# Experts of a decoder layer: result transposed, down weights in two parts, summed in PSUM, gates multiplied into silu's output

## The chip, the cores and the metric

One core of one Trainium2 chip runs the whole kernel. The metric is device time in microseconds (us). Five engines work beside each other and meet at semaphores: PE (TensorE, matmuls; PEld is its weight load), DVE (VectorE), ACT (ScalarE), POOL (GpSimd) and SP (SyncE, which here only issues DMAs). Each engine takes its instructions strictly in the order in which they were written.

## The reference, cut to what matters

One decoder layer for 8 batches of 256 tokens with 128 features: self attention, cross attention to 512 context tokens, then a mixture of experts, each followed by a residual and a layer norm. Only the experts change:

```
probs = softmax(xf @ w_router); top_vals, top_idx = top_k(probs, 2)
gates = top_vals / sum(top_vals);  cw = scatter(gates over 8 experts)
h1 = xf @ w1[e]; h3 = xf @ w3[e]                  # 128 -> 256, 8 experts
y  = (silu(h1) * h3) @ w2[e]                      # 256 -> 128
out = sum_e cw[:, e] * y[e] + (silu(xf @ sw1) * (xf @ sw3)) @ sw2
x = layernorm(x + out)
```

The kernel computes all experts for all tokens and weights them with gates, of which all but two are zero. The shared expert (sw1, sw3, sw2) is number 0, the routed ones are 1 to 8, so there are NE = 9 per batch and 72 in all.

## The kernel before, in words

The self attention of all batches comes first, then the cross attention, then the experts, batch by batch. What an engine does is recorded by `emit(kind, b, par, i)`, and an `Order` sets the sequence: every kind has a due time within a batch, counted in experts, and an engine's instructions are sorted by it. The experts' stage has its Orders in `experts` (from L1206) and is started from the engines' blocks in `decoder_layer`.

An expert step before is this. PE does kind H: twelve matmuls (L1463 to L1465) of 128x256 in fp32r, which give h1 and h3 transposed (hidden on the partitions, 256 tokens on the free axis). Every product is made of three, since the up weights and the tokens are each held as a rounded part and a rest ("hi" and "lo", fp32r). ACT takes silu of h1 (L1333), DVE multiplies by h3 (L1411) into `hidden`. PE does kind Y, two experts later (LAG = 2): four matmuls (L1472) of 128x128 in fp32, two tiles of 128 tokens times two halves of the hidden axis (eight records in the trace, since each runs in two passes), with `hidden` as the stationary operand and `w_down` as the moving one, so that y has tokens on the partitions. DVE then adds y to `state`: the shared expert by L1423, each routed one by L1425, which multiplies by the token's gate (a scalar per partition). PSUM has three slots of two banks, and H and Y take them by turns.

After the ninth expert of a batch DVE takes statistics (L1431), POOL computes mean and root in a chain of twelve small instructions (L1287 to L1305, kind TAIL, in an Order of its own), DVE normalizes (L1403, kind NORM), and SP stores. POOL has nothing else to do in the stage but for its beginning: there it makes the rests of the up weights of experts 3 to 8 (L1276, kind UP) and the chain of the cross attention's last layer norm (L819 to L841, kind N3). The top-2 choice (kind ROUTE, 18 DVE instructions with one ACT exp in between, L1327) is made once for batches 0 to 6 during the last cross attention and once for batch 7 in the experts' first two batches.

Of the kernel before, what the change touches and what calls it, by code (L numbers as in the profile page):

```python
# [123 lines left out]
def decoder_layer(nc, x, ctx, mask, wq, wk, wv, wo, g1, b1, g2, b2, xwq, xwkv, xwout,  # L124
# [28 lines left out]
    with top:  # L153
# [45 lines left out]
        m.room, m.powers = early.vals, early.powers  # L199
# [15 lines left out]
        with nc.Block() as block:  # L215
# [8 lines left out]
            @block.gpsimd  # L224
            def _(pool):
                emit, more = c.gpsimd(pool), e.gpsimd(pool)
                a.gpsimd(pool, {last: steps(emit, "N1", 5, 0, 1) + steps(emit, "N2", 5, 9, 1),
                                B: steps(emit, "Y", 1, 9, 1)})
                c.pool_order.run(emit, {1: steps(more, "UP", r.FIRST, 3, 2)}, done=("N1", "N2", "Y"),
                                 left=[("N3", last), ("XLO", last)])  # L230
                for at in range(r.FIRST, r.FIRST + 2):
                    more("UP", 0, 0, at)
                for at in range(5):
                    emit("N3", last, last % 2, at)
                for at in range(r.FIRST + 2, NE):
                    more("UP", 0, 0, at)
                more("XLO", last, last % 2, 0)
                e.tail_order.run(more)

            @block.scalar  # L240
            def _(act):
                emit, more = c.scalar(act), e.scalar(act)
                a.scalar(act, {B: steps(emit, "TX", 1, 5, 1) + steps(emit, "TC", 1, 5, 1)})
                c.act_order.run(emit, {1: steps(more, "UP", r.FIRST, 2, 2), last: steps(more, "EXP", 1, 27, 1), B: steps(more, "H", r.AHEAD, 5, 1)},
                                done=("TX", "TC"))
                for at in range(r.FIRST, NE):
                    more("UP", 0, 0, at)
                e.order.run(more, left=ahead, between={0: [(6.75, lambda: more("XT", last, last % 2, 0))], 1: [(0.5, lambda: more("EXP", 1, 0, 0))]})

            @block.vector  # L250
            def _(dve):
# [16 lines left out]
            @block.tensor
            def _(pe):
# [3 lines left out]
                e.order.run(more, left=ahead, between={0: [(6.5, lambda: more("XT", last, last % 2, 0)), (8, lambda: more("LOGITS", last, last % 2, 0))]})  # L273
# [3 lines left out]
def between_stages(nc, sem, sb, mem, m):  # L277
# [21 lines left out]
    r.gates = sb(mem, "gates", [P, tiles, E])  # L299
# [394 lines left out]
def cross_early(mem, sb, m):  # L694
# [5 lines left out]
    e.ctx_in = sb(mem, "ctx_in", [P, 2, CT, D])  # L700
# [5 lines left out]
    e.normed = sb(mem, "normed", [P, KT, D])  # L706
    e.y = sb(mem, "y", [P, KEYS])
# [9 lines left out]
def cross_attention(nc, sem, sb, ps, slot, m, r, mem, early, last_use):  # L717
# [173 lines left out]
    def scalar(act):  # L891
        def emit(kind, b, par, i):
            if kind in ("TC", "TX") and b < B:
# [5 lines left out]
                                     scale=gb[:, g:g + 1], bias=gb[:, g + 1:g + 2]).then_inc(ready, 1)  # L899
            if kind == "TX" and b >= 2:  # L900
# [289 lines left out]
    c.heads_ready = heads_ready, B * PAIRS  # L1190

# [10 lines left out]
def experts(nc, sem, sb, ps, slot, m, r, c, mem):  # L1202
# [41 lines left out]
    slots = Turns(order, full, SLOTS, c.free)  # L1244
# [263 lines left out]
```

## Time and profile before

| | us |
|---|---|
| median of 3 runs | 1153.52 (1153.27 to 1154.64) |
| the profiled execution | 1154.32 |
| its span in the trace | 1152.5 |
| PE busy in the span | 1104.0 (96%) |
| DVE, ACT, POOL busy | 879.1, 735.5, 539.6 |
| granted TensorE clock, mean | 0.996 of full speed |

Times of rows count from the span's start. A matmul's duration in the trace holds its way through the array, and matmuls overlap: what one costs is the distance from its start to the next start. A group's row gives the mean duration of one. An instruction's duration on DVE or POOL also holds the time in which it has been started and cannot go on.

### The profile page before, as it was taken

The page shows a single profiled execution, that of the slowest core. Times are in us where ns is not written, and L with a number is a line of the kernel's source. Part 1 is how long each engine was busy: PE and PEld are TensorE (multiplying, and loading weights), DVE is VectorE, ACT ScalarE, POOL GpSimd, SP SyncE. Part 2 cuts the span into 40 slices and gives each one's busy share as a digit, 9 for nine tenths or more (in the row PEclk, how much of TensorE's full clock was granted, in tenths as well). Part 3 has the DMA queues.
Part 4 walks back from the last instruction along what each step waited for, and adds up shares of the span by engine and source line. Part 5 has one row for each costly group of instructions (what it writes and reads, how often), then busy time and mean ns, then how long its engine had stood idle before and what let it go on. Part 6 is the DMA issues. An engine that isn't in the chain of part 4 may idle for free. (4 is left out here: it accounts for less than half of the span.)

```text
span 1152.5 us, 27526 instructions
## 1 busy us (share of the span) xinstructions
PE 1104.0 (96%) x8781; PEld 946.9 (82%) x8781; DVE 879.1 (76%) x2786; ACT 735.5 (64%) x1754; POOL 539.6 (47%) x892
## 2 busy tenths in 40 slices
PE   6999997999999999999999999999999998999997
PEld 5888875778888887887888888888788887999997
DVE  7999996888878788778787878877878685655554
ACT  6999996667757666666765766666667565322221
POOL 4666665554574355446456445544644432400101
PEclk9999999999999999999999999999999999999999
DMA  2000011000000000000000000000000003000000
GB/s 92 7 7 11 7 44 38 1 11 1 2 1 11 2 1 11 1 1 11 2 1 1 11 2 1 2 1 2 1 2 1 2 1 96 3 10 6 11 6 11
DMA packets 14685, 12.39 MB, mean 11 GB/s; under 512 B 1361, under 2 KB 13649, under 8 KB 14417
## 3 DMA queue, kind: packets, MB, share of 16 engines
q1 hardware_dynamic: 14128, 10.43, 3.0%
q8 instruction: 75, 1.23, 0.4%
q14 instruction: 66, 0.53, 0.2%
q10 hardware_dynamic: 416, 0.20, 0.1%
HBM read 9.57 MB, written 1.05 MB: 9 GB/s over the span
## 5 line engine op out<-in xcount | busy, mean ns | idle before, releaser
L874 POOL TENSOR_TENSOR xk_parts<-k_raw,xk_parts 64x768 fp32r<-64x768 f32 x128 | 236.1, 1845 | 312.7 <-DVE xk_parts L992 310.0
L1016 DVE CUSTOM_DVE_ANT_0 xmasked<-ps,bar 128x768 f32<-128x768 f32 x256 | 244.3, 954 | 4.2 <-issue 0.6
L1128 PE MATMUL ps<-xk_parts,xq_parts 128*128 128x512 f32 (+1 forms) x1024 | 233.2, 350 | 6.9 <-DVE xq_parts L997 3.4
L929 ACT ACTIVATE xprobs<-xmasked,xlow 128x768 f32<-128x768 f32 x256 | 238.0, 930 | 1.4 <-DVE xlow L1016 1.4
L1134 PE MATMUL ps<-ident,xprobs 128*128 128x128 f32 x1536 | 215.0, 276 | 7.1 <-DVE xlow L1016 6.0
L1128 PEld LDWEIGHTS ps<-xk_parts,xq_parts 128*128 128x128 f32 x1024 | 174.4, 189 | 33.3 <-DVE xq_parts L997 3.8
L1134 PEld LDWEIGHTS ps<-ident,xprobs 128*128 128x128 f32 x1536 | 168.9, 140 | 16.7 <-DVE xlow L1016 10.8
L1145 PE MATMUL ps<-xprobs_t,xvals 128*64 128x256 f32 x1536 | 179.9, 383 | 1.1 <-ACT xprobs_t L935 1.1
L1145 PEld LDWEIGHTS ps<-xprobs_t,xvals 128*64 128x64 f32 x1536 | 104.8, 137 | 57.9 <-issue 10.6
L1021 DVE COPY xprobs_t<-ps 128x768 f32<-128x768 f32 x128 | 121.6, 950 | 3.5 <-PE ps L1134 3.5
L909 ACT ACTIVATE k_raw<-ps 128x768 f32<-128x768 f32 x64 | 52.0, 812 | 105.1 <-PE ps L1102 94.3
L1333 ACT ACTIVATE xvals<-ps 128x512 f32<-128x512 f32 x72 | 42.9, 597 | 115.4 <-PE ps L1465 114.2
L115 DVE MEMSET xspare<- 128x1 f32 x256 | 15.1, 59 | 132.8 <-issue 111.4
L497 ACT ACTIVATE probs<-masked,low 128x128 f32<-128x128 f32 (+1 forms) x256 | 114.6, 458 | 0.0
L935 ACT ACTIVATE xprobs_t<-ps 128x768 f32<-128x768 f32 x128 | 103.0, 805 | 4.1 <-PE ps L1134 2.6
L1411 DVE TENSOR_TENSOR xvals<-ps,xvals 128x512 f32<-128x512 f32 x72 | 49.7, 691 | 69.0 <-ACT xvals L1333 69.0
L941 ACT ACTIVATE xrsum_t<-ps 128x256 f32<-128x256 f32 x64 | 24.6, 385 | 112.1 <-PE ps L1153 112.1
L451 POOL TENSOR_TENSOR q_head<-q_parts,head_of 128x256 fp32r<-128x256 f32 x128 | 76.2, 613 | 31.5 <-DVE q_parts L560 31.5
L570 DVE CUSTOM_DVE_ANT_0 masked<-ps,causal 128x128 f32<-128x128 f32 (+1 forms) x256 | 79.5, 353 | 0.0
L921 ACT ACTIVATE xvals<-ps 128x768 f32<-128x768 f32 x64 | 52.0, 812 | 41.0 <-PE ps L1120 41.0
L1472 PE MATMUL ps<-w_down,xvals 128*128 128x128 f32 x576 | 75.9, 275 | 1.1 <-DVE xvals L1411 1.1
L1472 PEld LDWEIGHTS ps<-w_down,xvals 128*128 128x128 f32 x576 | 70.2, 191 | 1.5 <-DVE xvals L1411 1.5
(220 smaller groups left out, 2524.8 us busy)
## 6 DMA issues: line engine op xcount, KB each, us to landing
ctx_in<-in_ctx SPq DMA_DIRECT2D x8, 256.0 KB, 3.3
w_rest<-in_L_ffn_w SPq DMA_DIRECT2D x2, 768.0 KB, 6.4
raw_kv<-in_L_xattn_Wkv SPq DMA_DIRECT2D x1, 1024.0 KB, 5.3
out<-state SPq DMA_DIRECT2D x8, 128.0 KB, 2.0
x_in<-in_x SPq DMA_DIRECT2D x7, 128.0 KB, 2.2
raw_q<-in_L_xattn_Wq SPq DMA_DIRECT2D x1, 512.0 KB, 6.1
wout<-in_L_xattn_Wout SPq DMA_DIRECT2D x1, 512.0 KB, 3.9
keep_all<-in_mask_BxS_bk SPq DMA_DIRECT2D x1, 512.0 KB, 4.7
```

Of the source, the lines that this page charges most:

```text
L451: pool.tensor_tensor(q_head[:, i % 4, :], q_parts[:, g % 2, :].bitcast(F32), head_of[:, i % HG:i % HG + 1].broadcast_to([P, S]), ALU.mult) ...
L497: nc.scalar.activation(probs[:, i % 4, lo:hi], masked[:, r, lo:hi], ACT.Exp, scale=-1.0, bias=low[:, r, j:j + 1], accum_out=sums[:, g % 2, ...
L570: dve.tensor_tensor_reduce(masked[:, r, lo:hi], bank(s, hi - lo, j * S), causal[:, S - (hi - lo):S], 1.0, 3e38, ALU.add, ALU.min, low[:, r ...
L874: pool.tensor_tensor(k_parts[dst, i // 2 % 2, h, :], k_raw[src, :], k_parts[src, i // 2 % 2, h, :].bitcast(F32), ALU.subtract).then_inc(k_ ...
L929: nc.scalar.activation(probs[:, i % 4, :], masked[:, i % 4, :], ACT.Exp, scale=-1.0, bias=low[:, i % 4:i % 4 + 1], accum_out=sums[:, pair ...
L935: nc.scalar.activation(probs_t[:, i % 4, :, 0, :], slot(slots.place("PT", 2 * i), KEYS).rearrange("p (k t) -> p k t", k=KT), ACT.Copy).the ...
L1016: dve.tensor_tensor_reduce(masked[:, i % 4, :], slot(slots.place("S", i), KEYS), bar[:, par, :], 1.0, 3e38, ALU.add, ALU.min, low[:, i % 4 ...
L1021: dve.tensor_copy(probs_t[:, i % 4, :, 1, :], slot(slots.place("PT", 2 * i + 1), KEYS).rearrange("p (k t) -> p k t", k=KT)).then_inc(pt_dv ...
L1128: last = nc.tensor.matmul(slot(s, hi - lo, lo), q_parts[:, pair % 2, h, part, t * P:(t + 1) * P], k_parts[:, pair % 2, h, lo:hi], start=pa ...
L1134: last = nc.tensor.transpose(slot(s, P, j * P), probs[:, i % 4, j * P:(j + 1) * P], ident[:, :])
L1145: last = nc.tensor.matmul(ps[h * XD:(h + 1) * XD, O_BANK + i % 2, 0:S], vals[:, i // 2 % 2, j, c:c + XD], probs_t[:, (2 * i + h) % 4, j, : ...
L1472: last = nc.tensor.matmul(slot(s, D, j * D), hidden[:, i % 3, k * S + j * P:k * S + (j + 1) * P], w_down[:, i, k, :], start=(k == 0), stop ...
```

## The change

The result of an expert is now transposed: `w_down` is the stationary operand, `hidden` the moving one, in fp32r in three products as H has them, so Y is six matmuls of 128x256. For that `w_down` and `hidden` are each split in a rounded part and a rest: the weights once (kind DOWN, ACT L1408 and DVE L1508), hidden for every expert (kind HI on ACT, L1433, and kind LO on DVE, L1522). All nine experts of a batch add up in one PSUM bank; then ACT copies the sum out (SUM, L1437), PE transposes it back (BACK, L1606), and DVE adds it to `state` (ADD, L1529), once per batch.

A gate per token can no longer be a scalar per partition. So the gates are transposed by PE, written to DRAM, and read back broadcast to all partitions (`load_wide`, 1 MB per batch, into the rooms of the attention's `k_parts` and `q_parts`), and POOL multiplies them into silu's output before DVE's H multiplies by h3 (kind GATE, L1361). The shared expert has no GATE. In batch 7 the shared expert comes last.

The choice is now made for batches 0 to 5 and for 6 and 7. Y's lag is three experts. TAIL is cut in five pieces that stand among the GATEs. The rests of the up weights of experts 3, 5, 7 are made by DVE, those of 4, 6, 8 by POOL. `w_down` is loaded earlier, during the last cross attention, into the room of `ctx_in`, `normed` and `y`.

```diff
-    LAG = 2
-    order = Order(B, NE, {"H": (NE, 0), "Y": (NE, LAG)})
-    dve_order = Order(B, NE, {"H": (NE, 0), "Y": (NE, LAG), "NORM": (1, NE + LAG + 2.25)})
-    tail_order = Order(B, NE, {"TAIL": (1, NE + LAG + 2.5)})
+    LAG = 3
+    END = NE + LAG
+    order = Order(B, NE, {"H": (NE, 0), "Y": (NE, LAG), "BACK": (1, END + 1.5)})
+    dve_order = Order(B, NE, {"H": (NE, 0), "LO": (NE, 0.95), "ADD": (1, END + 1.9), "NORM": (1, END + 5.9)})
+    act_order = Order(B, NE, {"H": (NE, 0), "HI": (NE, 1.5), "SUM": (1, END + 0.6)})
+    pool_order = Order(B, NE, {"GATE": (NE, 0.75), "TAIL": (5, END + 2.8, 0.65)})
...
+    def load_wide(sp, b):
+        sp.wait_ge(rows_written, 16 if b < r.EARLY else 32)
+        if b < 2:
+            sp.wait_ge(*c.scored)
+        else:
+            sp.wait_ge(weighted, E * (b - 1))
+        wait(sp, loaded_wide, 16 * b)
+        n = E * T
+        sp.dma_start(wide[b % 2], r.gate_rows[b * n:(b + 1) * n, :].rearrange("(e t) p -> e (t p)", e=E).partition_broadcast(P)
+                     ).then_inc(loaded_wide, 16)
...
+            if kind == "GATE" and expert(b, i) > 0:
+                n, e = b * NE + i, expert(b, i)
+                pool.wait_ge(silu_done, n + 1)
+                pool.wait_ge(loaded_wide, 16 * (b + 1))
+                values = silu[:, i % RING, :].rearrange("p (k s) -> p k s", k=HB)
+                pool.tensor_tensor(values, values, wide[par][:, e - 1:e, :].broadcast_to([P, HB, S]), ALU.mult
+                                   ).then_inc(weighted, 1)
...
+            if kind == "HI":
+                act.wait_ge(hidden_ready, n + 1)
+                wait(act, y_full, n - RING + 1)
+                nc.scalar.activation(hidden_hi[:, i % RING, :], hidden[:, i % RING, :], ACT.Copy).then_inc(hi_done, 1)
+            if kind == "SUM":
+                act.wait_ge(y_full, (b + 1) * NE)
+                nc.scalar.activation(summed_t[:, par, :], ps[:, O_BANK + par, 0:S], ACT.Copy).then_inc(sum_out, 1)
...
             if kind == "H":
                 dve.wait_ge(silu_done, n + 1)
-                wait(dve, full["Y"], n - 2)
-                dve.tensor_tensor(hidden[:, i % 3, :], slot(s, HB * S, BANK),
-                                  silu[:, i % 3, :], ALU.mult).then_inc(hidden_ready, 1)
-            if kind == "Y":
-                for j in range(T):
-                    tokens, y = state[:, b * T + j, :], slot(s, D, j * D)
...
-                        dve.scalar_tensor_tensor(out=tokens, in0=y, scalar=gates[:, b * T + j, i - 1:i], in1=tokens,
-                                                 op0=ALU.mult, op1=ALU.add).then_inc(summed, 1)
+                if expert(b, i) > 0:
+                    dve.wait_ge(weighted, weights_before(b, i))
+                wait(dve, split, n - RING + 1)
+                dve.tensor_tensor(hidden[:, i % RING, :], slot(s, HB * S, BANK),
+                                  silu[:, i % RING, :], ALU.mult).then_inc(hidden_ready, 1)
+            if kind == "LO":
+                dve.wait_ge(hi_done, n + 1)
+                wait(dve, y_full, n - RING + 1)
+                dve.tensor_tensor(hidden_lo[:, i % RING, :], hidden[:, i % RING, :],
+                                  hidden_hi[:, i % RING, :].bitcast(F32), ALU.subtract).then_inc(split, 1)
+            if kind == "ADD":
+                dve.wait_ge(back_full, b + 1)
+                dve.tensor_tensor(tokens, ps[:, O_BANK + par, S:S + T * D].rearrange("p (t d) -> p t d", t=T), tokens,
+                                  ALU.add).then_inc(summed, 1)
...
             if kind == "Y":
-                for j in range(T):
-                    for k in range(HB):
-                        last = nc.tensor.matmul(slot(s, D, j * D),
-                                                hidden[:, i % 3, k * S + j * P:k * S + (j + 1) * P],
-                                                w_down[:, i, k, :], start=(k == 0), stop=(k == HB - 1))
+                pe.wait_ge(down_ready, i + 1 if b == 0 else NE)
+                pe.wait_ge(split, n + 1)
+                o = ps[:, O_BANK + par, 0:S]
+                for k in range(HB):
+                    nc.tensor.matmul(o, wh, xh, start=(i == 0 and k == 0), stop=False)
+                    nc.tensor.matmul(o, wh, xl, start=False, stop=False)
+                    last = nc.tensor.matmul(o, wl, xh, start=False, stop=(i == NE - 1 and k == HB - 1))
```

How the instructions stand on POOL in an ordinary batch of the experts' stage before; the names are the small statistics of the layer norm, and the next batch's chain follows at once:

```order
L1287 TENSOR_TENSOR n_gap<-n_stats 128x2
L1288 TENSOR_TENSOR n_var<-n_stats 128x2
L1289 TENSOR_TENSOR n_sum<-n_stats 128x2
L1291 TENSOR_TENSOR n_fix<-n_gap 128x2
L1292 TENSOR_SCALAR n_var<-n_var 128x2
L1293 TENSOR_SCALAR n_mean<-n_sum 128x2
L1295 TENSOR_TENSOR n_var<-n_var,n_fix 128x2
L1297 TENSOR_TENSOR n_root<-n_var,x_powers 128x2
```

POOL in an ordinary batch of the change (`xvals` is the room of silu's output, `xq_parts` and `xk_parts` the rooms of the broadcast gates; L1361 is GATE):

```order
L1361 TENSOR_TENSOR xvals<-xvals,xq_parts 128x512 x5
L1369 TENSOR_TENSOR n_gap<-n_stats 128x2
L1370 TENSOR_TENSOR n_var<-n_stats 128x2
L1371 TENSOR_TENSOR n_sum<-n_stats 128x2
L1374 TENSOR_TENSOR n_fix<-n_gap 128x2
L1375 TENSOR_SCALAR n_var<-n_var 128x2
L1376 TENSOR_SCALAR n_mean<-n_sum 128x2
L1378 TENSOR_TENSOR n_var<-n_var,n_fix 128x2
L1361 TENSOR_TENSOR xvals<-xvals,xq_parts 128x512
L1381 TENSOR_TENSOR n_root<-n_var,x_powers 128x2
L1361 TENSOR_TENSOR xvals<-xvals,xq_parts 128x512
L1384 TENSOR_TENSOR n_fix<-n_root 128x2
```

The chain of the batch before now stands between the GATEs of experts 5 to 8, and what is queued behind a GATE waits for it. DVE in the middle of a batch before, from one expert to the next, with the end of the batch before it (statistics, first expert's addition):

```order
L1411 TENSOR_TENSOR xvals<-ps,xvals 128x512
L1425 SCALAR_TENSOR_TENSOR state<-ps,gates,state 128x128 x2
L1429 MEMSET n_spare 128x1
L1431 BN_STATS n_stats<-state 128x6 x2
L1411 TENSOR_TENSOR xvals<-ps,xvals 128x512
L1423 TENSOR_TENSOR state<-ps,state 128x128 x2
```

DVE at the same place of the change (L1516 is H, L1522 LO with `y_hi` and `y_lo` as the rooms of hidden's two parts, L1529 ADD):

```order
L1516 TENSOR_TENSOR xvals<-ps,xvals 128x512
L1529 TENSOR_TENSOR state<-ps,state 128x256
L1532 MEMSET n_spare 128x1
L1534 BN_STATS n_stats<-state 128x6 x2
L1522 TENSOR_TENSOR y_lo<-xvals,y_hi 128x512
L1516 TENSOR_TENSOR xvals<-ps,xvals 128x512
L1522 TENSOR_TENSOR y_lo<-xvals,y_hi 128x512
```

The two gated additions of every expert are gone, and an expert's LO stands between its own H and the next one's, so DVE's next H cannot start before ACT's HI and the LO of the expert before are done. The beginning of the stage on DVE in the change (L1503 makes rests of up weights, L1508 those of down weights, L1061 adds the cross attention's result):

```order
L1516 TENSOR_TENSOR xvals<-ps,xvals 128x512
L1503 TENSOR_TENSOR rest_lo<-w_rest,rest_hi 128x2x256
L1522 TENSOR_TENSOR y_lo<-xvals,y_hi 128x512
L1061 TENSOR_TENSOR state<-ps,state 128x256
L1065 BN_STATS stats<-state 128x6 x2
L1508 TENSOR_TENSOR down_lo<-front,down_hi 128x256 x2
L1516 TENSOR_TENSOR xvals<-ps,xvals 128x512
L1503 TENSOR_TENSOR rest_lo<-w_rest,rest_hi 128x2x256
L1508 TENSOR_TENSOR down_lo<-front,down_hi 128x256
L1522 TENSOR_TENSOR y_lo<-xvals,y_hi 128x512
```

Twelve weight splits stand among DVE's work of the first batch, where there were none.

## Rows read from the trace of the kernel before

**Rows 1.** The page, part 1: busy us, share of span, instructions
```profile
PE 1104.0 (96%) x8781; PEld 946.9 (82%) x8781; DVE 879.1 (76%) x2786; ACT 735.5 (64%) x1754; POOL 539.6 (47%) x892
```

**Rows 2.** Windows of one batch: length, busy by engine, clock, DMA
```profile
1024.90:1045.45 20.55, 20.55 (x182) 20.55 (x182) 11.73 (x33) 5.37 (x9) 2.80 (x12) 1.00 0.03 8
...
1107.15:1127.72 20.57, 20.57 (x183) 20.57 (x182) 11.75 (x33) 5.37 (x9) 2.80 (x12) 1.00 0.03 8
```

**Rows 3.** Chain that ended last: start, us, what; Y's of three batches
```profile
982.27 0.90 PE ps L1472 x8
...
1024.89 0.90 PE ps L1472 x8
...
1045.45 0.90 PE ps L1472 x8
```

**Rows 4.** Timeline of PE, one H and its neighbours: start, us
```profile
987.67 0.28 PE L1464 MATMUL ps<-cxt_lo,rest_hi 128*128 128x256 f32 x1
...
988.92 1.05 PE L1472 MATMUL ps<-w_down,xvals 128*128 128x128 f32 x8
```

**Rows 5.** Groups, 960 to the end: count, busy us, mean ns, idle before
```profile
L1411 DVE TENSOR_TENSOR xvals<-ps,xvals 128x512 f32<-128x512 f32 x72 | 49.7, 691 | 69.0 <-ACT xvals L1333 69.0
L1333 ACT ACTIVATE xvals<-ps 128x512 f32<-128x512 f32 x72 | 42.9, 597 | 115.4 <-PE ps L1465 114.2 <-issue 1.2
L1276 POOL TENSOR_TENSOR rest_lo<-w_rest,rest_hi 128x512 fp32r<-128x512 f32 x6 | 7.5, 1276 | 9.7 <-ACT rest_hi L1318 9.7
L1318 ACT ACTIVATE rest_hi<-w_rest 128x512 fp32r<-128x512 f32 x6 | 3.2, 616 | 0.2 <-issue 0.2
```

**Rows 6.** Groups of POOL over the whole span, one input broadcast
```profile
L451 POOL TENSOR_TENSOR q_head<-q_parts,head_of 128x256 fp32r<-128x256 f32 x128 | 76.2, 613 | 31.5 <-DVE q_parts L560 31.5
```

**Rows 7.** Timeline of POOL and DVE, two pairs that overlap
```profile
988.61 1.27 POOL L1276 TENSOR_TENSOR rest_lo<-w_rest,rest_hi 128x512 fp32r<-128x512 f32 x1
988.66 1.30 DVE L1050 TENSOR_SCALAR state<-state,r_mean,r_root 128x128 f32<-128x128 f32 x1
...
950.04 1.84 POOL L874 TENSOR_TENSOR xk_parts<-k_raw,xk_parts 64x768 fp32r<-64x768 f32 x1 [3.56 <-DVE xk_parts L992]
951.58 0.44 DVE L1361 TENSOR_TENSOR scratch<-scratch,index 128x112 f32<-128x112 f32 x1
```

**Rows 8.** Timeline of DVE, a like instruction with POOL idle
```profile
954.26 0.27 DVE L1365 TENSOR_TENSOR chosen<-index,first 128x112 f32<-128x112 f32 x1
```

**Rows 9.** Timeline, a small POOL instruction behind a DVE cast
```profile
334.19 0.55 DVE L992 CAST xk_parts<-k_raw 64x768 fp32r<-64x768 f32 x1
...
334.23 0.56 POOL L828 TENSOR_TENSOR r_var<-r_var,r_fix 128x2 f32<-128x2 f32 x1
```

**Rows 10.** Chain that ended last, the last batch's end
```profile
1141.37 0.04 issue
1141.42 0.60 ACT xvals L1333
...
1142.79 2.07 PE ps L1472 x16
1144.94 0.61 DVE state L1425 x2
...
1146.15 0.20 POOL n_gap L1287
...
1149.66 0.35 DVE state L1403
```

**Rows 11.** Timeline of ACT around the second choice
```profile
999.60 1.28 ACT L1327 ACT_TABLE_LOAD   x1
...
1001.32 1.28 ACT L1333 ACT_TABLE_LOAD   x1
```

**Rows 12.** The page, part 6: DMA issues, KB each, us to landing
```profile
raw_kv<-in_L_xattn_Wkv SPq DMA_DIRECT2D x1, 1024.0 KB, 5.3
```

More of the change, by code:

```diff
@@ new lines, in _ @@
+                e.dve_order.run(more, left=ahead[:1] + [("LO", 0, 0)], between={
+                    0: [(0.5 + 0.5 * i, lambda i=i: more("DOWN", 0, 0, i)) for i in range(NE)]
+                    + [(at, lambda i=i: more("UP", 0, 0, i)) for i, at in ((5, 1.2), (7, 3.2))],
+                    1: [(7.5, lambda: emit("NORM2", last, last % 2, 0))],
+                    2: [(7.25, lambda: more("XHI", last, last % 2, 0)),
+                        (8.25, lambda: more("LOGITS", last, last % 2, 0))],
+                    3: [(0.5 + 0.3 * n, lambda n=n: more("ROUTE", 1, 0, n)) for n in range(r.STEPS)]})
@@ L272, in _ @@
                 c.pe_order.run(emit, {B: steps(more, "H", r.AHEAD, 2, 1)}, done=("TX", "TC"))
-                e.order.run(more, left=ahead, between={0: [(6.5, lambda: more("XT", last, last % 2, 0)), (8, lambda: more("LOGITS", last, last % 2, 0))]})
+                e.order.run(more, left=ahead, between={
+                    2: [(6.5, lambda: more("XT", last, last % 2, 0)), (8, lambda: more("LOGITS", last, last % 2, 0))],
+                    4: [(7, lambda: more("GATES", 0, 0, 0))]})
         e_mem.close()
@@ L298, in between_stages @@
     r.gate = sb(mem, "gate", [P, 2, tiles])
[L299 removed]
+    r.gates = sb(mem, "gates", [P, B, E, T])
+    r.gates_t = sb(mem, "gates_t", [P, 2, P])
+    r.gate_rows = nc.dram_tensor("gate_rows", [B * E * T, P], F32, kind="Internal").ap()
+    r.EARLY = 6
+    r.chain, r.gates_out = sem("r_chain"), sem("r_gates_out")
     r.moments = [sb(mem, "r_" + n, [P, T]) for n in ("gap", "total", "var", "fix", "mean", "root")]
@@ L899, in emit @@
                                      scale=gb[:, g:g + 1], bias=gb[:, g + 1:g + 2]).then_inc(ready, 1)
+            if kind == "TX" and b == B:
+                act.wait_ge(full["TX"], b + 1)
+                rows = r.EARLY * E * T
+                nc.scalar.activation(r.gates_t[0:rows, 0, :], slot(slots.place("TX", 0), P)[0:rows, :], ACT.Copy
+                                     ).then_inc(r.gates_out, 1)
             if kind == "TX" and b >= 2:
@@ L1080, in emit @@
                     last = nc.tensor.transpose(slot(s, P, n * P), normed[:, j, :], ident[:, :])
+            if kind == "TX" and b == B:
+                pe.wait_ge(r.chain, r.STEPS)
+                nc.tensor.transpose(slot(s, P)[0:r.EARLY * E * T, :],
+                                    r.gates[:, 0:r.EARLY, :, :].rearrange("p b e t -> p (b e t)"), ident[:, :])
             if kind == "TX" and b >= 2:
@@ L1380, in route @@
             if n == 17:
-                last = dve.tensor_tensor(gates[:, tiles, :], chosen[:, 0, tiles, :], chosen[:, 1, tiles, :], ALU.add)
-            last.then_inc(chain, 1)
+                first_b, end_b = (n // T for n in groups[g])
+                one, two = (chosen[:, k, tiles, :].rearrange("p (b t) e -> p b e t", t=T) for k in range(2))
+                last = dve.tensor_tensor(gates[:, first_b:end_b, :, :], one, two, ALU.add)
+            last.then_inc(r.chain, 1)
         def emit(kind, b, par, i):
```

290 lines of the change are left out of this document (179 added, 111 removed).

## The prediction

> **What bounds the kernel now.** I read the shares by engine first, then windows of single batches, then the chain that ended last, and then the groups of the experts' stage. PE is busy for 96% of the span [rows 1]. In the experts' stage it is all of the time: in two batches far apart PE is busy for 20.55 of 20.55 and 20.57 of 20.57 us at a granted clock of 1.00, while DVE has 11.7 us, ACT 5.4 and POOL 2.8 [rows 2]. The chain confirms it: the first batch's Y of expert 0 starts at 982.27, that of the third at 1024.89, the fourth's at 1045.45 [rows 3]. At 20.57 per batch the first pair would be 41.14 apart; it is 42.62, so 1.5 us of waits stand in the first two batches, and from there on a batch costs what PE works. So less work on PE is worth its full price, but only for as long as what feeds PE keeps up. Before, ACT and DVE stand between an H and its Y, and both are idle more than half of the time; the change puts POOL among them and gives DVE and ACT a second turn.
>
> **PE's work.** Eleven matmuls of an H take 988.92 − 987.67 = 1.25 us, 0.114 each, and a Y 0.90 [rows 3, 4]. After, Y is six matmuls of H's shape: 6 × 0.117 = 0.70 (0.114 is measured; the stationary operand of half of them differs, so I take up to 0.119). 72 × (0.90 − 0.70) = 14.4 us less. BACK adds two transposes per batch, at most H's price each: 16 × 0.11 = 1.8. Net −12.6 us, between −13.7 and −11.5 for a Y of 0.68 to 0.71. A batch would be 20.57 − 1.8 + 0.22 = 19.0 us, an expert 12 × 0.114 + 0.70 = 2.07.
>
> **What feeds PE.** Durations [rows 5]: silu 0.60; DVE's H 0.69; HI, an ACT copy of 128x512, 0.62 as the one of L1318; LO on DVE, of H's size, 0.69; GATE on POOL, as the subtraction of 128x512 at L1276, 1.28, or 1.24 back to back. GATE's second input is broadcast, and POOL's 128x256 with such an input takes 0.61 [rows 6], twice that 1.23; so 1.24, and 1.04 as a lower bound if the fixed part of it is 0.2. Per batch: POOL 8 × 1.24 + 3.5 of TAIL (1146.15 to 1149.66, [rows 10]) = 13.4; DVE 9 × 1.38 and the additions and norm, below 15; ACT 9 × 1.22 + a SUM of at most 0.60, 11.6. None of it is over 19.0. The sums do not bind; what can is the order.
>
> Two loops matter. First, PE's H of expert i+3 needs the PSUM slot of i, which DVE's H frees. From the end of H(i) to there PE has three Y and two H, 2.1 + 2.74 = 4.8 us; silu takes 0.64 of it, and 4.1 are left for GATE 1.24, DVE's H 0.69 and, with hops and a DVE that is just at the LO before, about 2.6 in all. The slack is 1.5 us. Y(i) has H(i+3) more, 1.37, for HI and LO, about 1.4: the same slack. Second, LO(i) stands on DVE ahead of H(i+1), and waits for ACT's HI(i): 0.69 + 0.62 + 0.69 and two hops are about 2.05 per expert. That is PE's own 2.07, so a lag that has once arisen is not worked off by DVE.
>
> **Whether DVE and POOL disturb each other.** GATE reads two operands from SBUF, and so does LO; DVE's H reads one from PSUM. The trace has such pairs. A DVE instruction on SBUF that started 0.05 after POOL's L1276 took 1.30 and ended 0.09 after it. A TENSOR_TENSOR of DVE with two SBUF inputs took 0.44 behind POOL's L874 and ended 0.13 after that [rows 7], where one of its kind took 0.27 with POOL idle [rows 8]. So DVE waits for POOL. The other way, a POOL instruction of 128x2 started at 334.23 beside a DVE cast and took 0.56, to 0.05 after the cast's end [rows 9], against 0.20 for such an instruction [rows 10]. That was a cast, not a two-input operation; no row has POOL starting under one of those. I take it that LO holds POOL as the cast did: for its elements, (0.69 − 0.27) / 400 = 1.05 ns each, 512 of them 0.54 us.
>
> The Trainium skill (SBUF — State Buffer, "Who interferes with whom") says that a DVE instruction with two SBUF inputs and a GpSimd instruction that reads SBUF share a port pair, which the first to start keeps until its end. The rows above agree where DVE comes second (1.30 and 0.44); for the case that POOL comes second behind a two-input DVE operation no row of this trace shows it, and by that page the sum is the one that follows, with the hold both ways.
>
> **An ordinary batch.** Between the end of GATE 5 and that of GATE 8 POOL has three GATEs and nearly all of TAIL, since its pieces stand among them: 3 × 1.24 + 3.5 = 7.2, and three LOs that hold it, 3 × 0.54 = 1.6, so 8.9 us. PE takes 6.2 for three experts. The 2.7 of excess less the slack of 1.5 leaves 1.2 us of idle PE per batch, which the DVE loop does not give back, over seven batches with a TAIL before them: +8.4. POOL itself does recover, in GATEs 1 to 4. Bounds: 0 if nothing is held, 1.9 per batch (+13) if hops cost more slack.
>
> **The first batches.** Twelve weight splits stand among DVE's work of batch 0: nine DOWN of 128x256 (elements 0.27, with the fixed part 0.42) and three UP of LO's size; POOL makes three UP, 3.7 us. What excludes each other in that batch is GATEs 9.9, POOL's UP 3.7, LOs 9 × 0.54 = 4.9, DOWN 9 × 0.27 = 2.4 and DVE's UP 1.6: 22.5 against 19.0, 3.5 too much; 1.5 more for the DVE loop, which has the splits in its way even with the port free: +5. Bounds: 1.5 with nothing held; 7 with whole durations held (0.69 and 0.42), which makes 25.7. In batch 1 POOL makes the layer norm of the cross attention's last batch, a chain like TAIL: +1. In batch 3 DVE makes the second choice, 18 small instructions, while ACT loads its table twice, 1.28 each [rows 11], and silu and HI are late by 2.6 at one blow, over a slack of 1.5: with DVE's 18 beside it +2.5 (bounds 1 and 4). Before, these cost 1.5 in batches 0 and 1, which goes.
>
> **The end.** Before, from the last H to the end of the sum it is 1141.37 to 1145.55, 4.2 us [rows 10]. After, batch 7 ends with the shared expert, without GATE, but expert 7's GATE comes about 1 late, then H, HI, LO of expert 7 (2.05), the same of expert 8 (2.05), Y 0.70, SUM 0.4, BACK 0.23, ADD 0.42 and hops 0.6: 7.5, so +3.3.
>
> **Costed at nothing.** The broadcasts are 1 MB per batch. A load of 1 MB landed in 5.3 us [rows 12], under 19 of a batch, with DMA at 3% [rows 2]; a batch's load starts when the GATEs two batches back are done. The load of w_down and the first gates' way through DRAM lie in the last cross attention, where DVE's and PE's work covers them. If the first broadcast were late, GATE(1) of batch 0 would stop everything once by what is missing.
>
> **Sum.** −12.6 + 8.4 + 5 + 1 + 2.5 + 3.3 − 1.5 = +6.1. The profiled execution took 1154.3, of which 1152.5 is span; with +6.1 that is 1160.4, and since it lay 0.8 above the median, 1159.6. I say 1160.
>
> **Rivals.**
> A: DVE and POOL do not disturb each other for these two kinds of operation. For it: DVE's H, with one operand in PSUM, is never longer beside POOL (691 on average of 72, [rows 5]). Against it: rows 7. Then POOL's window is 7.2 against 6.2 + 1.5, no stall; the splits cost 1.5, the choice 1.5 to 2, the end 3.3: −12.6 + 1.5 + 2 + 3.3 − 1.5 = −7.3, about 1147. This is the other side, and it decides at GATE 8: as soon as POOL's window is under 7.7, PE's gain stays.
> B: only DVE waits for POOL, as the two-input rows show, and a GATE is never held. POOL is in GATEs for 9.9 of 19.0 us, so half of the nine LOs meet one and wait for half of it, 0.62: at most 2.7 per batch where nothing hides it. The slack of 1.5 hides the first two, and expert 0, which has no GATE, regains some; I take 0.8, +6 over the batches, with splits +2.5: −12.6 + 6 + 2.5 + 2 + 3.3 − 1.5 = −0.3, about 1153.
> C: GATE is 1.04. The window is 0.6 shorter, 4 us over the batches less: 1156.
> D: both ways and no slack at all, with the upper ends (13, 7, 1, 4): −12.6 + 13 + 7 + 1 + 4 + 3.5 − 1.5 = +14.4, about 1168.
> E: the choice or the table loads hit a full pipe and cost nothing, which takes 2.5 from any of these.
>
> **How the numbers follow.** The forecast's mechanism, held both ways, 0.54 with C and D in it; A 0.30, as both views of the port are from a few rows; B 0.16. A is faster, and a sixth of the others with E; B is about the same; the rest slower. A difference of 0.2%, 2.3 us, is about what a measurement can tell from no change: faster 0.35, same 0.14, slower 0.51. The range takes in A below and D above: 1145 to 1170; the forecast's own is 1155 to 1168.
>
> **What will show it.** H at 0.114 and Y at 0.70 spacing, else the first term is wrong. LO's mean over 0.69, with its longest ones ending just behind a GATE, shows DVE held; GATE's mean over 1.24, with the longest (1.8) ending behind a LO, shows POOL held; both near 0.69 and 1.24 is rival A. The batch period is 19.0 under A, about 20.2 here. PE's idle time should stand before H 8 or the Ys after it, ended by DVE, and DVE's ended by POOL's GATE. In batch 0 the period should be near 24, in batch 3 near 22.7. I am wrong if PE is busy for 100% in ordinary batches, or if it stalls at every expert, which would put a loop over 2.07 in the place of TAIL.

## The result, and the profile after

The change takes 1165.34 us (median of 4 runs, 1165.15 to 1166.78) against 1153.47 before; the ratio is 1.0104, 95% interval 1.0086 to 1.0121. So it is slower, on the side that was forecast and inside the range, and by 11.9 us where 6.5 were forecast. The profiled execution took 1166.78 us, of which 1165.3 is span, and before's span was 1152.5. Busy time by engine after, page part 1, to set beside [rows 1]:

```profile
PE 1101.3 (95%) x8655; PEld 939.6 (81%) x8655; DVE 911.6 (78%) x2734; ACT 780.5 (67%) x1845; POOL 631.6 (54%) x953
```

PE is busy for less time, POOL for 92 us more, and the span is longer. The windows from one batch's first Y to the next one's (batches 0 to 6: length, then busy us and count of PE, PEld, DVE, ACT, POOL, then granted clock, DMA share, GB/s) answer to [rows 2]:

```profile
983.22:1010.93 27.71, 22.84 (x164) 22.19 (x163) 22.36 (x28) 13.79 (x27) 16.80 (x18) 0.88 0.12 40
1010.93:1031.65 20.72, 19.80 (x166) 19.26 (x165) 15.57 (x26) 9.83 (x18) 16.99 (x26) 1.00 0.11 32
1031.65:1053.02 21.37, 20.34 (x172) 19.93 (x171) 14.21 (x29) 10.95 (x20) 15.23 (x22) 1.00 0.16 58
1053.02:1077.29 24.27, 20.51 (x166) 19.51 (x165) 19.07 (x41) 13.00 (x22) 14.87 (x21) 1.00 0.16 53
1077.29:1097.62 20.33, 19.92 (x167) 19.54 (x166) 13.96 (x25) 10.83 (x20) 14.28 (x21) 1.00 0.08 30
1097.62:1117.95 20.33, 19.82 (x166) 19.27 (x165) 13.97 (x25) 10.68 (x19) 14.30 (x21) 1.00 0.19 77
1117.95:1138.17 20.22, 19.84 (x166) 19.39 (x165) 14.04 (x25) 10.68 (x19) 15.87 (x22) 1.00 0.11 43
```

An ordinary batch (the last three) is 0.24 to 0.35 us shorter than the 20.57 of before, where the matmuls alone would make it 19.1; batches 0 and 3 are far longer. Batch 0 was 22.05 before, by the same measure.

The timeline of batch 5 shows where the 1.2 us of an ordinary batch go. POOL first (start, duration):

```profile
1106.40 0.20 POOL L1378 TENSOR_TENSOR n_var<-n_var,n_fix 128x2 f32<-128x2 f32 x1
1106.55 1.74 POOL L1361 TENSOR_TENSOR xvals<-xvals,xq_parts 128x512 f32<-128x512 f32 x1
1108.25 0.72 POOL L1381 TENSOR_TENSOR n_root<-n_var,x_powers 128x2 f32<-128x2 f32 x1
1108.94 1.30 POOL L1361 TENSOR_TENSOR xvals<-xvals,xq_parts 128x512 f32<-128x512 f32 x1
1110.20 0.64 POOL L1384 TENSOR_TENSOR n_fix<-n_root 128x2 f32<-128x2 f32 x1
...
1111.61 1.30 POOL L1361 TENSOR_TENSOR xvals<-xvals,xq_parts 128x512 f32<-128x512 f32 x1
```

And DVE beside it, with what it waited for in brackets:

```profile
1106.45 0.69 DVE L1522 TENSOR_TENSOR y_lo<-xvals,y_hi 128x512 fp32r<-128x512 f32 x1 [0.70 <-ACT y_hi L1433]
1108.38 0.69 DVE L1516 TENSOR_TENSOR xvals<-ps,xvals 128x512 f32<-128x512 f32 x1 [1.24 <-POOL xvals L1361]
1109.76 1.02 DVE L1522 TENSOR_TENSOR y_lo<-xvals,y_hi 128x512 fp32r<-128x512 f32 x1 [0.70 <-ACT y_hi L1433]
1110.71 0.68 DVE L1516 TENSOR_TENSOR xvals<-ps,xvals 128x512 f32<-128x512 f32 x1
1112.09 1.38 DVE L1522 TENSOR_TENSOR y_lo<-xvals,y_hi 128x512 fp32r<-128x512 f32 x1 [0.70 <-ACT y_hi L1433]
```

Here POOL and DVE hold each other in both directions in one stretch. GATE 6 starts 0.10 after an LO and takes 1.74 instead of 1.30; the LO at 1109.76 starts in GATE 7 and takes 1.02, and n_fix, a POOL instruction of 0.19 us otherwise, starts in that LO and takes 0.64; the LO at 1112.09 starts in GATE 8 and takes 1.38. DVE's H of expert 6 waits 1.24 for its GATE. From the end of GATE 5 to that of GATE 8 it is 1104.60 to 1112.91, 8.3 us (8.9 forecast). PE's Y then finds its LO late:

```profile
1113.03 0.28 PE L1582 MATMUL ps<-cxt_hi,up_lo 128*128 128x256 f32 x1
1113.61 0.36 PE L1599 MATMUL ps<-y_hi,down_hi 128*128 128x256 f32 x1 [0.30 <-DVE y_lo L1522]
```

From start to start that is 0.58 instead of 0.12, and the Y before it had started 0.39 after its neighbour (1110.54 to 1110.93). Note that PE's busy column hides most of such a gap, since a matmul's record runs for 0.28.

In batch 0 PE stands idle three times, for 1.5, 1.3 and 2.9 us by its starts. Before the Y that ends the last of these, DVE has a DOWN split of 1.49 (0.42 where nothing holds it) and the LO of 1.74 that this Y waits for:

```profile
991.98 1.49 DVE L1508 TENSOR_TENSOR down_lo<-front,down_hi 128x256 fp32r<-128x256 f32 x1
993.39 1.74 DVE L1522 TENSOR_TENSOR y_lo<-xvals,y_hi 128x512 fp32r<-128x512 f32 x1
```

Behind this wait the granted clock falls to half. Windows of that stretch, same columns:

```profile
992.00:995.00 3.00, 0.66 (x6) 0.46 (x5) 3.00 (x3) 0.42 (x1) 2.59 (x2) 0.94 0.00 0
995.00:998.00 3.00, 2.71 (x13) 2.75 (x14) 2.63 (x6) 1.11 (x2) 0.70 (x1) 0.50 0.00 0
998.00:1001.00 3.00, 3.00 (x16) 3.00 (x16) 1.61 (x4) 1.79 (x3) 1.37 (x2) 0.50 0.00 0
1001.00:1004.00 3.00, 3.00 (x25) 3.00 (x25) 1.87 (x3) 1.12 (x2) 1.20 (x2) 0.92 0.00 0
```

At 0.50 (1.2 GHz) 27 matmuls stand 0.213 us apart instead of 0.118, 2.6 us.

The end, from the chain that ended last, answers to [rows 10]; three turns of H, HI, LO stand one behind the other, with H at 1149.15, 1151.46 and 1153.44:

```profile
1147.37 1.70 POOL xvals L1361
...
1149.15 0.70 DVE xvals L1516
1149.87 0.64 ACT y_hi L1433
...
1151.46 0.69 DVE xvals L1516
...
1153.44 0.69 DVE xvals L1516
...
1154.82 0.70 DVE y_lo L1522
...
1155.66 0.36 PE ps L1599
```

### The profile page after: what moved, and what is told of

Read it like the earlier page. It is cut to its first block and busy times, and to the rows that moved or that the text cites. A ratio compares the mean times of both kernels' runs of the same rounds, so it can differ in the third digit from the quotient of the medians.

```text
span 1165.3 us, 27569 instructions
## 1 busy us (share of the span) xinstructions
PE 1101.3 (95%) x8655; PEld 939.6 (81%) x8655; DVE 911.6 (78%) x2734; ACT 780.5 (67%) x1845; POOL 631.6 (54%) x953
## 5 line engine op out<-in xcount | busy, mean ns | idle before, releaser
L1433 ACT ACTIVATE y_hi<-xvals 128x512 fp32r<-128x512 f32 x72 | 45.5, 632 | 72.2 <-DVE xvals L1516 72.2
L1522 DVE TENSOR_TENSOR y_lo<-xvals,y_hi 128x512 fp32r<-128x512 f32 x72 | 61.3, 851 | 36.4 <-ACT y_hi L1433 36.2
L1013 DVE CAST xk_parts<-k_raw 64x768 fp32r<-64x768 f32 x128 | 70.6, 552 | 0.2 <-ACT k_raw L930 0.2
L654 PE MATMUL ps<-k_parts,q_head 128*128 128x256 f32 x256 | 62.6, 327 | 4.4 <-POOL q_head L465 1.8
```

The lines of the kernel that those rows point to most:

```text
L1013: dve.tensor_copy(k_parts[rows, i // 2 % 2, h, :], k_raw[rows, :]).then_inc(kh_done, 1)
```

## Experiments

Beside the medians each experiment is read by the length of its batches.

**The pair by itself.** The added part, at the end of the kernel, in short:

```diff
+    pool: tensor_tensor(w_rest[:, 0:2, j, :], silu, wide.broadcast, mult)           # x2 alone, then 3 x 6
+    dve:  tensor_tensor(lo, hidden, hidden_hi, subtract)                            # x2 alone, x8 beside
+    dve:  tensor_tensor(lo, ps, hidden_hi, subtract)  /  tensor_scalar(lo, hidden)  # x8 beside, each
```

> The change with a measurement added behind its end: GATEs of 128x512 (POOL) and DVE instructions of 128x512 that depend on nothing, first 2 GATEs alone, 2 LOs alone, then three stretches of 6 GATEs beside 8 instructions of DVE: LOs (two SBUF inputs), subtractions with one input in PSUM and one in SBUF, and TENSOR_SCALARs with one SBUF input. Theory (each holds the other for its elements): beside LOs a GATE takes 1.8 instead of 1.24 to 1.3 and an LO up to 1.9 instead of 0.69, the two take turns, and six pairs last about 6 x 1.8 = 10.8 us; beside the PSUM form both keep their durations alone (1.3 and 0.69). Rival A (no contention): 1.3 and 0.69 in all three. Rival B (only DVE waits): GATE 1.3 everywhere, LO stretched to over 1.2.

Groups of POOL beside LOs (first row), beside the PSUM form (second) and beside TENSOR_SCALARs (third), busy and mean ns; alone two took 2.48 us:

```profile
L1619 POOL TENSOR_TENSOR w_rest<-xvals,xk_parts 128x512 f32<-128x512 f32 x6 | 10.0, 1705 | 1.5 <-DVE y_lo L1636 1.5
...
L1619 POOL TENSOR_TENSOR w_rest<-xvals,xk_parts 128x512 f32<-128x512 f32 x6 | 7.4, 1259 | 1.2 <-DVE rest_lo L1642 1.2
...
L1619 POOL TENSOR_TENSOR w_rest<-xvals,xk_parts 128x512 f32<-128x512 f32 x6 | 8.5, 1449 | 0.1
```

And the timeline of DVE in the first stretch, in which the first LO and the last of the five were not held, and in the second:

```profile
1166.31 4.03 DVE L1642 TENSOR_TENSOR y_lo<-xvals,y_hi 128x512 fp32r<-128x512 f32 x3
1170.26 7.35 DVE L1642 TENSOR_TENSOR rest_lo<-xvals,y_hi 128x512 fp32r<-128x512 f32 x5
1177.64 1.89 DVE L1644 TENSOR_TENSOR y_lo<-ps,y_hi 128x512 fp32r<-128x512 f32 x3
1179.44 3.07 DVE L1644 TENSOR_TENSOR rest_lo<-ps,y_hi 128x512 fp32r<-128x512 f32 x5
```

The two take turns: six GATEs need 10.05 us, 1.67 for one with its LO, so an LO holds POOL for 0.44 (0.54 was forecast), and an LO takes 1.74. With one operand in PSUM both run as if alone: a GATE takes 1.26, and DVE's start 0.61 apart. That is the theory in both its halves; rivals A and B fall. A TENSOR_SCALAR on SBUF holds POOL as well, for 0.17.

**TAIL spread out.**

```diff
-    ... "NORM": (1, END + 5.9)})
+    ... "NORM": (1, END + 8.2)})
-    pool_order = Order(B, NE, {"GATE": (NE, 0.75), "TAIL": (5, END + 2.8, 0.65)})
+    pool_order = Order(B, NE, {"GATE": (NE, 0.75), "TAIL": (5, END + 2.8, 1.0)})
```

> TAIL's five pieces stand one expert apart instead of 0.65 (the last two beside expert 0, which has no GATE), and NORM 2.3 experts later. Nothing is left out. Theory (3 GATEs + the whole TAIL + holds in one window of POOL make the stall of 1.33 us per batch): with at most 1 us of TAIL ahead of any GATE the stall falls to 0 to 0.5 in batches 1, 2, 4, 5, 6 and part of 3; 1158 to 1161 us, period 19.0 to 19.5 in batches 4 to 6. Rival (the chain from silu to Y is too long for the lag, whatever stands on POOL, or DVE's loop of 1.99 sets the pace): period stays at 20.3, 1164.5 to 1166.

1159.37 us (ratio to before 1.0042, 1.0028 to 1.0056), 6 less than the change. Windows of batches 1, 3 and 5:

```profile
1012.19:1032.11 19.92, 19.61 (x166) 19.43 (x165) 15.69 (x24) 9.81 (x18) 17.40 (x26) 1.00 0.00 1
...
1052.41:1075.53 23.12, 20.51 (x166) 19.62 (x165) 19.18 (x41) 12.99 (x22) 15.22 (x21) 1.00 0.16 52
...
1095.09:1114.29 19.20, 19.20 (x166) 19.10 (x165) 14.37 (x24) 10.72 (x19) 14.56 (x21) 1.00 0.18 64
```

Batch 5 goes from 20.33 to 19.20 with the same work on every engine, and PE is busy throughout. So TAIL's place among the GATEs is the ordinary batch's stall (NORM, which needs TAIL's result, moved with it; the two are not parted here). Batch 3 loses as much and keeps the rest.

**GATE left out.**

```diff
-            if kind == "GATE" and expert(b, i) > 0:   # on POOL, with DVE's wait for it
```

> GATE is left out, so routed experts are added without their weights; all else as in the change. Theory (GATE on POOL, against LO and the splits, makes the stalls): batches 4 to 6 at 19.0, batch 0 at 20 to 22 with the clock at full speed, end 3 us shorter; 1145 to 1149 us. Rival (HI, LO and DVE's loop alone hold PE up): batches still over 20, 1158 or more.

The broadcasts then wait for H instead of GATE. 1146.09 us in its one run. Batches 0, 2, 3 and 6:

```profile
983.18:1003.67 20.49, 20.01 (x165) 19.38 (x163) 15.55 (x25) 12.95 (x27) 7.38 (x14) 1.00 0.15 54
...
1022.77:1042.66 19.89, 19.89 (x173) 19.89 (x171) 14.07 (x34) 10.61 (x20) 5.07 (x13) 1.00 0.18 61
1042.66:1062.04 19.38, 19.38 (x167) 19.38 (x165) 14.03 (x36) 12.86 (x22) 3.97 (x12) 1.00 0.15 48
...
1100.79:1119.87 19.08, 19.08 (x167) 19.08 (x165) 12.98 (x25) 10.63 (x19) 3.32 (x12) 1.00 0.03 9
```

Without GATE PE is never idle from batch 1 on, although HI, LO and the chain through ACT and DVE are all there. Batch 2 is longer than batch 6 with PE busy for all of it: the few records more are XT and LOGITS, the last batch's transposes and logits. What is left there is work, not a wait. Batch 3, which has the second choice and both table loads, is 19.38, as batches 4 and 5 are (19.37 and 19.38): without GATE the choice costs at most 0.3 us (batch 6 is 19.08).

**GATE on DVE.**

```diff
-    dve_order = Order(B, NE, {"H": (NE, 0), "LO": (NE, 0.95), ...
+    dve_order = Order(B, NE, {"H": (NE, 0), "GATE": (NE, -0.3), "LO": (NE, 0.95), ...
-                pool.tensor_tensor(values, values, wide[par][:, e - 1:e, :].broadcast_to(...), ALU.mult)
+                dve.tensor_tensor(values, values, wide[par][:, e - 1:e, :].broadcast_to(...), ALU.mult)
```

> GATE moves from POOL to DVE, between the H before and its LO, where DVE idles 0.70 us for HI. Nothing is left out. Theory (the stalls come from POOL's 1.3 us, from TAIL ahead of it and from the hold between POOL and DVE): DVE's turn per expert is 0.61 + 0.70 + 0.61 = 1.92 against PE's 2.07, GATE takes 0.61; batches 4 to 6 at 19.0 to 19.3, batch 0 about 23, end shorter by 2 to 3; 1147 to 1151 us. Rival (DVE is the bound: 26 x 0.61 + 1.6 = 17.5 us and the waits for HI in a batch of 19): batches at 20.5 or more, 1163 or more.

1149.94 us, ratio to before 0.9966 (0.9954 to 0.9977): faster than before, with the whole computation. Batches 0, 3 and 5:

```profile
983.52:1005.48 21.96, 20.45 (x165) 19.46 (x163) 20.86 (x35) 13.02 (x27) 8.05 (x14) 1.00 0.12 49
...
1044.61:1064.88 20.27, 19.72 (x166) 19.49 (x165) 18.64 (x45) 12.75 (x22) 4.66 (x12) 1.00 0.12 42
...
1084.26:1103.34 19.08, 19.08 (x167) 19.08 (x165) 17.92 (x33) 11.26 (x19) 4.42 (x12) 1.00 0.25 100
```

DVE is now busy for 17.9 of 19.08 and PE for all of it. The engine that looked too full is the better place, since a GATE there takes 0.61 from start to start, fills the time in which DVE waits for HI, and is not held (0.68 on average, as H). What it holds is TAIL on POOL: n_mean takes 0.76 instead of the 0.22 of the run without GATE, and POOL is busy for 4.4 us of a batch instead of 3.3, which PE does not feel. Batch 3 falls by 4.0 with the choice and both table loads in it.

**The down weights' rests left out, in a single run and in several.**

```diff
-                    0: [(0.5 + 0.5 * i, lambda i=i: more("DOWN", 0, 0, i)) for i in range(NE)]
...
-                pe.wait_ge(down_ready, i + 1 if b == 0 else NE)
+                pe.wait_ge(down_hi_done, i + 1 if b == 0 else NE)
...
-                    wh, wl = (... for a in (down_hi, down_lo))
+                    wh, wl = (... for a in (down_hi, down_hi))
```

> The nine DOWN splits of DVE are left out, and Y takes the rounded down weights in the place of their rests; ACT's part stays. Theory (in batch 0 DVE's splits take turns with POOL's GATE and UP: a sum of 22.5 us against 19.0, of which DOWN is 2.4 and its turns on DVE more; PE's waits of 5.6 us then drop the clock, which costs 3.0 more): batch 0 at 21 to 23 instead of 27.7, the clock at full speed all through it; 1159 to 1161 us. Rival (POOL's three UP ahead of the GATEs are what is late): batch 0 at 26 or more with the clock falling, 1163.5 or more.

1164.69 us in its one run, which fits neither: batch 0 was 21.75 as the theory has it, with the clock at 1.00 in it. The profile shows where it went back: from 150 to 230 us, long before the stage, the clock was 0.97 and 0.95 in two windows of 40 us, in which the change had 1.00, and the first Y started at 985.65 instead of 983.22. So it was run again, several times.

> The kernel without DVE's nine DOWN splits once more, timed in rounds, since its single run lay only 0.65 us below the change while its batch 0 took 21.75 us. Theory (the splits take 3.3 us of batch 0, and what the single run lost, 2.4 us, it lost ahead of the stage): 1161 to 1163 us. Rival (what batch 0 gains is lost elsewhere in every run): 1164.3 or more.

1162.05 us (1.0071, 1.0059 to 1.0084), with batch 0 at

```profile
983.57:1005.46 21.89, 19.64 (x165) 19.27 (x163) 14.46 (x19) 13.23 (x27) 16.72 (x18) 1.00 0.14 48
```

**The change again, on the same chip.**

> The change itself, beside the next two on the same chip. Theory and rivals alike: 1165.0 to 1165.7 us. In its profile batch 0 is 27.7 us if the clock falls there again, about 25.0 if it doesn't, as in the run without table loads, whose batch 0 has the same code.

1167.09 us (1.0112, 1.0096 to 1.0127), 1.75 more than the first time and outside what was expected. Its batch 0, and the stretch in which PE stands idle:

```profile
985.47:1010.52 25.05, 20.18 (x164) 19.42 (x163) 20.59 (x27) 12.98 (x27) 16.53 (x18) 1.00 0.12 43
994.00:997.00 3.00, 0.91 (x9) 0.71 (x7) 3.00 (x3) 0.67 (x2) 2.84 (x2) 1.00 0.00 0
997.00:1000.00 3.00, 2.47 (x19) 2.39 (x20) 2.63 (x6) 1.12 (x2) 0.45 (x1) 1.00 0.00 0
```

PE stands idle for the same 2.9 us, and the clock does not fall; batch 0 is 25.05. So the stalls of batch 0 cost 6 us over 19.1 in every profile, DVE's DOWN splits 3.2 of it (25.05 to 21.89), and the clock's 2.7 on top are not in every run. In this run the clock fell elsewhere: from 150 to 230 us (0.96 and 0.95), after which the first Y came 2.2 us later than in the first profile of the same kernel, and in the end, where the last two Ys and the transposes ran at half clock and the end took 27.9 us instead of 27.1. The run without DOWN's rests, on the same chip, is 5.0 us faster than this one: 3.2 of it is batch 0, and 1.9 stands ahead of the first Y in the profiles, where this run had the lower clock.

**No table load in batch 3.**

```diff
-                nc.scalar.activation(gap[:, lo:hi], gap[:, lo:hi], ACT.Exp)
+                nc.scalar.activation(gap[:, lo:hi], gap[:, lo:hi], ACT.Copy if b else ACT.Exp)
```

> The exponential of the second choice (batches 6 and 7) is left out, a copy stands in its place, so that ACT loads no table in batch 3. Theory (two loads of 1.28 us at one blow, over the slack, are most of batch 3's excess): batch 3 at 21.3 to 22.3 instead of 24.3, 1162 to 1163.5 us. Rival (the choice's DVE instructions, held by GATE, and SUM queued behind HI are the excess, the loads lie beside them): batch 3 at 23.5 or more, 1164.5 to 1166.

1165.26 us, and batch 3 is 24.09 instead of 24.27:

```profile
1050.74:1074.83 24.09, 20.39 (x167) 19.50 (x165) 20.14 (x41) 10.43 (x20) 14.70 (x21) 1.00 0.16 56
```

The rival holds: the two loads of 1.28 us cost 0.2.

**No second choice.**

```diff
-                    3: [(0.5 + 0.3 * n, lambda n=n: more("ROUTE", 1, 0, n)) for n in range(r.STEPS)]})
+                    3: [(0.5 + 0.3 * 17, lambda: more("ROUTE", 1, 0, 17))]})
```

> Seventeen of the eighteen DVE instructions of the second choice and its exponential are left out; the last one writes gates of earlier batches in the place of those of batches 6 and 7. Theory (DVE's choice, held by GATE, and SUM and BACK queued behind it are batch 3's excess): batch 3 at 20.3 to 20.8 instead of 24.2, 1161.2 to 1162.2 us. Rival (batch 3's excess is the lag that XT, XLO and LOGITS leave at the end of batch 2): batch 3 at 22.5 or more, 1163.5 or more.

1161.60 us (1.0067, 1.0055 to 1.0080), and batch 3 is an ordinary one:

```profile
1050.68:1071.15 20.47, 19.81 (x167) 19.26 (x165) 14.21 (x26) 10.68 (x19) 14.42 (x21) 1.00 0.19 67
```

The choice costs 3.8 us with GATE on POOL (0.2 of it the table loads, which went with its exponential) and at most 0.3 with GATE left out. The change's own timeline of DVE shows how: an instruction of 128x32 is caught behind the GATE that runs from 1054.56 to 1056.13, and H behind it:

```profile
1054.90 1.28 DVE L1470 SCALAR_TENSOR_TENSOR logits<-chosen,logits 128x32 f32<-128x32 f32 x1
1056.10 0.68 DVE L1516 TENSOR_TENSOR xvals<-ps,xvals 128x512 f32<-128x512 f32 x1
```

ACT's HI follows at 1056.82, SUM, which stands behind it, at 1057.35, and PE, whose next instruction is BACK, starts it 1.97 us after the matmul before. SUM needed nothing of that HI; it stood behind it. This wait is about half of the 3.8; the others of that batch are two of 1.1 us, before a Y that waits for LO and an H that waits for DVE's H.

**Better versions.** On top of GATE on DVE, LO one place later (H, LO of the expert before, GATE), everywhere:

```diff
-    ... "LO": (NE, 0.95), ...
+    ... "LO": (NE, 1.05), ...
```

> GATE on DVE as in the kernel that moved it there, and LO one place later: H(i), LO(i-1), GATE(i+1). Nothing is left out. Theory (DVE's 0.70 us of waiting for HI goes from its turn, which then is 3 x 0.61 = 1.83 per expert; batch 0 is bound by DVE's sum, the end by the loop H, HI, LO): batch 0 at 21.0 to 21.6 instead of 21.95, batch 3 at 19.3 to 19.8, end 0.6 to 1.2 shorter; 1147 to 1148.8 us. Rival (Y gets its LO 1.2 us later, and now waits for it): batches over 19.5, 1151 or more.

1150.72 us (0.9967, 0.9955 to 0.9980), no better, and between the two forecasts. Batch 0 is 22.74 and batch 3 21.17, longer than with LO early: Y now waits for its LO there (PE's starts are up to 1.6 us apart), as the rival has it, but not in the ordinary batches (19.1 to 19.4). From the last batch's first Y to the end it is 24.1 instead of 26.1. With four DOWN splits on POOL as well:

```diff
-                    ... lambda i=i: more("DOWN", 0, 0, i)) for i in range(NE)]           # DVE
+                    ... lambda i=i: more("DOWN", 0, 0, i)) for i in (0, 1, 3, 5, 7)]     # DVE
+                    ... for i, at in ((2, 0.9), (4, 2.8), (6, 5.8), (8, 6.8))]             # POOL
```

> As the run before it, and four of the nine DOWN splits go from DVE to POOL. Nothing is left out. Theory (batch 0 is bound by DVE: 4 x 0.33 us less there, but each split on POOL, 0.73, can hold up a GATE or LO of DVE): batch 0 between 20.3 and 21.5, 1146.3 to 1148.5 us. Rival (holds give back all and more): batch 0 at 22 or more, 1148.5 to 1150.

1151.46 us (0.9976, 0.9967 to 0.9986). The rival held, and the time lies above its range too: batch 0 is 23.37, with a wait of 2.7 us before the Y of expert 1 and fifteen matmuls at half clock behind it. So LO late only where it gained:

```diff
+ left=[("LO", last, i) for i in range(NE)]
+ last: [(i + 1.05, lambda i=i: more("LO", last, last % 2, i)) for i in range(NE - 1)]   # the ninth at B: 0.05
```

> GATE on DVE as in the run that moved it, and LO one place later in the last batch alone. Nothing is left out. Theory (LO late costs 0.8 in batch 0 and 0.9 in batch 3, but shortens the end by 2, as the run with LO late everywhere showed part by part): 1147.6 to 1149 us. Rival (the shorter end was the clock's, not LO's place): 1149.6 or more.

1148.96 us (1147.70 to 1149.41), ratio to before 0.9955 (0.9942 to 0.9967): 4.9 us under before and 16 to 18 under the change. It has the lowest median of all, though its interval overlaps that of GATE on DVE alone (0.9954 to 0.9977), so what LO's place adds is not settled by the times. From the last batch's first Y to the end it is 24.1 again; of the 2.0 to the 26.1 before some 0.9 is clock, since the last Y's six matmuls and the transposes stood at half clock in the end of the run with LO early (2.9 us from that Y's start to ADD, 1.95 here).

## Why the prediction was right, and what it mis-sized

**PE's work, −12.6.** Right. Matmuls of both kinds stand 0.114 to 0.120 apart, and with PE never idle a batch takes 19.07 to 19.38 (19.0 forecast). Why the same matmuls stand 0.114 apart in some batches and 0.118 in others stayed open.

**POOL and DVE hold each other.** Right, and shown in both directions by the pair alone. The step that rested on a cast [rows 9] carried over to LO; the hold is 0.44, not 0.54. Of [rows 7] only the row of 0.44 had two tensor inputs in SBUF, as LO has; that of 1.30 was a TENSOR_SCALAR with one, a kind that the pair alone shows to take turns with POOL as well.

**An ordinary batch, 1.2 each.** Right: 20.33 − 19.07 = 1.26. The run with TAIL spread out shows that it is the window of three GATEs and TAIL. That the holds tip it is worked out, not shown by a run of its own: of the window's 8.3 us they are 0.44 on GATE 6, about 0.4 on n_gap (0.57) and 0.45 on n_fix, 1.3 in all, and without them it would be 7.0, under the 7.7 at which the prediction puts the limit.

**The first batch, +5.** Right in kind: 25.05 − 19.07 = 6.0 without the clock, of which DOWN is 3.2. What the sum lacked is that PE, once it has stood idle, may get the lower clock: 2.7 more in the profiled run.

**"Silu and HI are late by 2.6 at one blow".** This step failed. Batch 3 costs 5.2 over 19.07 where 3.7 were forecast, and the table loads, which I put in as its main part, are 0.2. It is the choice's small instructions on DVE, which cost at most 0.3 with GATE left out (19.38), and each of which a GATE can now hold for up to 1.1 us (1.28 instead of 0.19); behind them DVE's H, HI, SUM and BACK come late. The sum held LO and the splits against GATE, but not these.

**"Before, these cost 1.5 in batches 0 and 1, which goes".** Failed in part. I took the whole distance between Y's over 20.57 [rows 3] for waits. 0.8 of it is PE's own work, XT and LOGITS, and it moved to batch 2 (19.89 with PE busy throughout, against 19.08), which came to 21.37.

**The end, +3.3.** Of the right kind, too small: the sum has two turns of H, HI and LO behind a late GATE, the chain has three. From the last batch's first Y to the end of the span it was 24.9 before. PE's saving leaves 22.0 of that (nine cheaper Y, two transposes, and H 3 now stands ahead of that Y); it is 27.1, so 5.1 more, where 3.3 and a TAIL window of 1.2 were forecast.

**The transfers and the gates' way through DRAM, 0.** Right. The 1 MB broadcasts land in 4.8 to 5.2 us, [rows 12] for a like one, and by the profile one GATE waited for one, 0.7 us, no longer than the GATEs beside it waited for silu.

Added up against before's span: −12.1 for PE's work (counted to the last batch's end), 8.6 − 1.5 in batch 0, 1.7, 2.3, 5.2, then 1.3, 1.3, 1.2, the end 5.1, and −0.2 ahead of the first Y (H 3 now stands before it): +12.9 of the 12.8 measured.

## What to carry to other kernels

An engine's busy share does not say what an added instruction costs there: with GATE on POOL, which had 18 of 20 us free, the change lost 12 us, and with GATE on DVE, which is then busy for 94% of a batch, it won 4. Ask which operands the instruction has, which instructions of the other engine it will run beside, and what is queued behind it. Before a difference of two starts is called a wait, count the instructions in between.

## What the runs showed of the hardware that was not expected

The fall of the clock is no fixed price of a stall. PE stood idle for the same 2.9 us in batch 0 in several runs of the same code; in two profiles (the change, and TAIL spread out) 27 matmuls at 0.50 followed, and in three others (the change again, no table load, no second choice) none. Nor does a fall always cost time. In the run with the pair added behind the end, whose batch 0 has the same code, it came one wait earlier: twelve matmuls at half clock took 1.0 us more, the next wait was 1.9 instead of 2.9, and batch 0 was 25.09 again. What PE lost ahead of its wait for DVE, the wait gave back. In the second run without DOWN's rests it fell behind 2.0 us of idle PE in batch 3, which the change has too, without a fall. A change of 2 to 3 us in a single run of this kernel can be that alone, as the run without DOWN's rests showed.

A DVE TENSOR_SCALAR with a single SBUF input takes turns with POOL too (1.40 us per pair against 1.24 for POOL alone), though it holds it for less than half as long as one with two inputs.
